# Last stage of an audio tower: column groups of 144, 512 and 512, first norms made one stage earlier, the last tile's router columns first

## The reference, cut to what matters

```python
h = h + attn(layernorm(h), ...)             # its last product: o @ wo.T
x = layernorm(h)
base_out = x @ base_W.T + base_b            # 1024 -> 1024
logits = x @ router_W.T + router_b          # 15 columns
p = softmax(logits); topk_p, topk_i = top_k(p, 8)
w[e] = sum of topk_p with expert_map[topk_i] == e
lora = ((x @ A.T) * w) @ B * 2              # 8 experts of rank 16
h = h + base_out + lora
```

## Time and profile before

| what | value |
|---|---|
| median of three runs | 2515.33 us |
| profiled execution, its own time | 2515.87 us |
| span of the profile | 2514.2 us |
| mean granted TensorE clock | 0.976 |
| TensorE busy | 2367.1 us, 94% of the span |
| VectorE busy | 1807.6 us, 72% |
| ScalarE busy | 1247.0 us, 50% |
| GpSimd busy | 1234.2 us, 49% |

### The profile page before, as it was taken

How to read it: one execution, slowest core, us unless ns; L and a number is a source line. 1 busy time by engine, 2 the same in 40 slices (tenths; PEclk the granted TensorE clock), 3 DMA queues, 4 the chain that set the end, 5 groups by cost and what they waited for, 6 DMA issues and landing times. The chain is left out here.

```text
span 2514.2 us, 45922 instructions
## 1 busy us (share of the span) xinstructions
PE 2367.1 (94%) x14716; PEld 2056.5 (82%) x14716; DVE 1807.6 (72%) x3550; ACT 1247.0 (50%) x3736; POOL 1234.2 (49%) x1012
## 2 busy tenths in 40 slices
PE   8999999988699996899999999989999997999998
PEld 6888878866466676899999999878888875999998
DVE  8865586795456666888888898755776556777775
ACT  5664354441344555899999999823223222111110
POOL 5764686784022224876676767610676553111110
PEclk9999999999899998999999999989999998999999
DMA  7654587666656552211111111197788996211111
GB/s 249 206 178 124 183 260 239 217 217 211 222 168 212 185 177 80 74 43 49 42 49 45 45 46 41 47 309 229 212 254 244 293 274 223 71 68 68 67 67 50
DMA packets 318257, 379.44 MB, mean 151 GB/s; under 512 B 25472, under 2 KB 260480, under 8 KB 317952
## 3 DMA queue, kind: packets, MB, share of 16 engines
q1 hardware_dynamic: 310176, 348.10, 44.2%
q0 software_dynamic: 7184, 25.69, 2.6%
q10 hardware_dynamic: 720, 3.67, 0.4%
HBM read 295.59 MB, written 81.79 MB: 150 GB/s over the span
## 5 line engine op out<-in xcount | busy, mean ns | idle before, releaser
L1518 ACT ACTIVATE attn_prob<-attn_prob,attn_bias 94x94 f32<-94x94 f32 x1024 | 366.9, 361 | 44.4 <-DVE attn_bias L1597 43.1
L740 PE MATMUL up_ps<-up_t_lo,up_s_hi 128*128 128x502 f32 (+1 forms) x840 | 332.9, 396 | 24.4 <-DVE up_t_lo L655 24.4
L741 PE MATMUL up_ps<-up_t_hi,up_s_lo 128*128 128x502 f32 (+1 forms) x840 | 329.2, 392 | 0.0
L742 PE MATMUL up_ps<-up_t_hi,up_s_hi 128*128 128x502 f32 (+1 forms) x840 | 328.5, 391 | 0.0
L506 POOL TENSOR_TENSOR up_both<-up_raw 128x502 f32<-128x502 f32 (+1 forms) x150 | 240.9, 1610 | 114.0 <-DVE up_t_lo L655 83.3
L1638 POOL TENSOR_TENSOR attn_prob<-attn_prob,attn_share 94x752 f32<-94x752 f32 x128 | 187.1, 1462 | 173.7 <-DVE attn_share L1605 173.7
L1886 DVE TENSOR_TENSOR out_t_lo<-early_raw,out_t_hi 128x512 fp32r<-128x512 f32 x168 | 159.1, 951 | 151.1 <-ACT out_t_hi L1865 150.2
L1851 POOL TENSOR_TENSOR early_raw<-early_raw 128x512 f32<-128x512 f32 x120 | 172.1, 1439 | 194.7 <-DMA early_raw<-o_t 193.7
L1865 ACT ACTIVATE out_t_hi<-early_raw 128x512 fp32r<-128x512 f32 x168 | 105.0, 631 | 305.2 <-POOL early_raw L1851 148.8
L655 DVE TENSOR_TENSOR up_t_lo<-up_both,up_t_hi 128x502 fp32r<-128x502 f32 (+1 forms) x150 | 164.3, 1097 | 83.8 <-ACT up_t_hi L564 82.3
L2026 POOL TENSOR_TENSOR ffn_res<-shared_k_t,ffn_bias 128x1024 f32<-128x1024 f32 x24 | 58.7, 2448 | 316.1 <-DVE ffn_o L2148 295.8
(11 more groups left out here) (238 smaller groups left out, 6368.8 us busy)
## 6 DMA issues: line engine op xcount, KB each, us to landing
early_raw<-o_t SPq DMA_DIRECT2D x288, 256.0 KB, 5.0
up_raw<-x_f SPq DMA_DIRECT2D x240, 251.0 KB, 3.3
up_w_raw<-w SPq DMA_DIRECT2D x120, 256.0 KB, 4.0
up_raw<-x_f SPq DMA_DIRECT2D x120, 250.0 KB, 3.6
shared_ring<-wvo SPq DMA_DIRECT2D x96, 256.0 KB, 5.1
o_t<-attn_o_t SPq DMA_DIRECT2D x128, 188.0 KB, 1.9
shared_ring<-wo SPq DMA_DIRECT2D x32, 512.0 KB, 6.6
y<-early_raw POOLq DMA_DIRECT2D x24, 512.0 KB, 3.5
```

What stands on the lines that cost most here:

```text
L740: nc.tensor.matmul(o, sh, tl, start=(kk == 0), stop=False)
L741: nc.tensor.matmul(o, sl, th, start=False, stop=False)
L742: last = nc.tensor.matmul(o, sh, th, start=False, stop=(kk == KH - 1))
L1518: last = nc.scalar.activation(prob[u % NPR][0:SEQ, h, part], prob[u % NPR][0:SEQ, h, part], ACT.Exp, bias=bias[u % 2][0:SEQ, n:n + 1], sca ...
```

## The change

1. **Column groups.** `CUT` goes from [0, 390, 780, 1168] to [0, 512, 1024, 1168], and `base` takes the groups in the order 2, 0, 1: 144 columns (A, router, padding), then 512, then 512. The LoRA product and `ffn_o` now have two groups of 512 in place of 390, 390 and 244.
2. **First norms.** `attn_out` makes the norm's moments of tile 1 ahead of its step 148 and of tile 0 ahead of its step 152, and `xn` of tile 0 as well, into a buffer that outlives the stage and that `c_t` of tile 3 uses before. In `ffn` the first step makes no norm, and the second makes only `xn` of tile 1.
3. **Order of the splits in `ffn`.** ScalarE splits block 0 of `wf` after the first four transposes, and blocks 1 to 8 after both `xt_hi`; VectorE splits blocks 0 and 1 after its first `xt_lo` and 2 and 3 after its second. Before, both engines split blocks 0 to 3 ahead of any of this (VectorE after tile 0's norm).
4. **Residual sums.** GpSimd's first three `res` wait for tile 0's base product.
5. **Last tile.** Its group of 144 columns is done first for all eight blocks (so `base_made` comes then), and the two groups of 512 follow; the LoRA product of the tile before stands after block 4 and not after block 6.

```diff
-def attn_out(nc, d, ow, ox, wf, tiles, h_in):
+def attn_out(nc, d, ow, ox, wf, tiles, h_in, begun):
...
-        c_t = tiles + [mem.sb(f"c_t{i}", [P, DM])[:] for i in range(len(tiles), TILES)]
+        c_t = tiles + [begun.xn] + [mem.sb(f"c_t{i}", [P, DM])[:] for i in range(len(tiles) + 1, TILES)]
...
+            def norm(t):
+
+                dve.wait_ge(taken, PAIR * FINAL_HIGH + t + 1)
+                link.step(1 - t)
+                moments(nc, link, c_t[t], bn, begun.vec[t])
+                link.fill()
+                if t == 0:
+                    dve.wait_ge(lent_stored, 16)
+                    nc.vector.tensor_scalar(begun.xn, c_t[0], begun.vec[0][:, 8:9], begun.vec[0][:, 11:12],
+                                            ALU.subtract, ALU.mult)
+
             for s in range(STEPS):
+                if s in (24 * FINAL_LOW + 4, 24 * FINAL_LOW + 8):
+                    norm(1 - (s - 24 * FINAL_LOW - 4) // 4)
                 dve.wait_ge(hi_done, s + 1)
...
-CUT = [0, 390, 780, FW]
+CUT = [0, DM // 2, DM, FW]
...
                     if not first(t, 3):
                         pool.wait_ge(o_done, t - 2)
+                    else:
+                        pool.wait_ge(base_made, 1)
...
-            for n in range(EARLY):
-                wf.split_hi(act, n)
...
                         act.wait_ge(x_turned, 2 * t + c + 1)
+                        if first(t, 1) and c == 0:
+                            wf.split_hi(act, 0)
...
                     if first(t, 1):
-                        for n in range(EARLY, KM + 1):
+                        for n in range(1, KM + 1):
                             wf.split_hi(act, n)
...
+                        if first(t, 1):
+                            for n in range(2 * c, 2 * c + 2):
+                                wf.split_lo(dve, n)
...
                     if first(t, 1):
-                        for n in range(EARLY):
-                            wf.split_lo(dve, n)
+                        dve.sem_inc(xn_done, 1)
+                    else:
+                        if first(t, 2):
+                            v = begun.vec[1]
+                        else:
+                            v = vec
+                            moments(nc, link, hh, bn, v)
...
-                    for c in range(3):
-                        a, e = CUT[c], min(CUT[c + 1], DM)
+                    for c in range(2):
+                        a, e = CUT[c], CUT[c + 1]
...
-            def base(s, blocks):
+            def base(s, blocks, groups=(2, 0, 1)):
...
-                if n == KM - 1:
+                if n == KM - 1 and 2 in groups:
                     last.then_inc(base_made, 1)
...
-                    base(s, range(0, 4))
+                    ending = isinstance(s[0], int) and s[0] == TILES - 1
+                    groups = (0, 1) if ending else (2, 0, 1)
+                    before = 5 if ending else 7
+                    if ending:
+                        base(s, range(KM), (2,))
+                    base(s, range(0, 4), groups)
...
-                    base(s, range(4, 7))
+                    base(s, range(4, before), groups)
...
-                    base(s, range(7, KM))
+                    base(s, range(before, KM), groups)
```

More of the change, by code:

```diff
@@ L1775, with __init__, moments @@
 ]
-def attn_out(nc, d, ow, ox, wf, tiles, h_in):
+class Begun:
+    def __init__(self, nc, mem):
+        self.xn = mem.sb("xn0", [P, DM])[:]
+        self.vec = [mem.sb(f"vec{i}", [P, 16])[:] for i in range(2)]
+def moments(nc, link, h, bn, v):
+    nc.vector.bn_stats(bn[:, 0:6], h[:, 0:512])
+    link(nc.vector.bn_stats(bn[:, 6:12], h[:, 512:1024]))
+    link.settle()
+    link(nc.vector.bn_aggr(v[:, 8:10], bn[:]))
+    link(nc.vector.tensor_scalar(v[:, 10:11], v[:, 9:10], LN_EPS, None, ALU.add))
+    inv_sqrt(nc, link, v[:, 10:11], v[:, 13:14], v[:, 11:12], v[:, 12:13])
+def attn_out(nc, d, ow, ox, wf, tiles, h_in, begun):
     NT, NB = 5, 8
@@ L1783, in attn_out @@
         ow.more(mem)
-        c_t = tiles + [mem.sb(f"c_t{i}", [P, DM])[:] for i in range(len(tiles), TILES)]
+        c_t = tiles + [begun.xn] + [mem.sb(f"c_t{i}", [P, DM])[:] for i in range(len(tiles) + 1, TILES)]
+        bn = mem.sb("bn", [P, 12])
+        link_sem = mem.sem("link")
+        lent_stored = mem.sem("lent_stored")
         t_hi = [mem.sb(f"t_hi{i}", [P, 4, P], F32R) for i in range(NT)]
@@ L1843, in _ @@
                 sp.sem_inc(h_in[t], 16)
-            sp.wait_ge(h_stored, 16 * TILES)
+            sp.wait_ge(h_stored, 16 * (TILES - 1))
+            sp.wait_ge(lent_stored, 16)
         @block.gpsimd
@@ L1940, in ffn @@
         o = [mem.sb(f"o{i}", [P, DM]) for i in range(2)]
-        xn = [mem.sb(f"xn{i}", [P, DM]) for i in range(2)]
+        xn = [begun.xn, mem.sb("xn1", [P, DM])]
         xt_hi = [mem.sb(f"xt_hi{i}", [P, KM, P], F32R) for i in range(2)]
@@ L2120, in body @@
                     dve.wait_ge(h_in[u % 3], 16 * nth(kb, u, 3))
-                    nc.vector.bn_stats(bn[:, 0:6], hh[:, 0:512])
-                    link(nc.vector.bn_stats(bn[:, 6:12], hh[:, 512:1024]))
-                    link.settle()
-                    link(nc.vector.bn_aggr(vec[:, 8:10], bn[:]))
-                    link(nc.vector.tensor_scalar(vec[:, 10:11], vec[:, 9:10], LN_EPS, None, ALU.add))
-                    inv_sqrt(nc, link, vec[:, 10:11], vec[:, 13:14], vec[:, 11:12], vec[:, 12:13])
-                    if not first(t, 2):
-                        dve.wait_ge(x_turned, 2 * t - 2)
-                    nc.vector.tensor_scalar(xn[u % 2][:], hh[:], vec[:, 8:9], vec[:, 11:12], ALU.subtract,
-                                            ALU.mult).then_inc(xn_done, 1)
-                    if first(t, 1):
-                        for n in range(EARLY):
-                            wf.split_lo(dve, n)
+                    if first(t, 1):
+                        dve.sem_inc(xn_done, 1)
[5 more added lines that the diff above has]
+                            moments(nc, link, hh, bn, v)
+                        if not first(t, 2):
+                            dve.wait_ge(x_turned, 2 * t - 2)
+                        nc.vector.tensor_scalar(xn[u % 2][:], hh[:], v[:, 8:9], v[:, 11:12], ALU.subtract,
+                                                ALU.mult).then_inc(xn_done, 1)
                     if isinstance(t, int) and t == 1:
@@ L2168, in base @@
                         wf.wait(pe, n)
-                    last = three_pass(nc, [ps_o[u % 2][c][:, 0:CUT[c + 1] - CUT[c]] for c in range(3)],
+                    last = three_pass(nc, [ps_o[u % 2][c][:, 0:CUT[c + 1] - CUT[c]] for c in groups],
                                       xt_hi[u % 2][:, n, :], xt_lo[u % 2][:, n, :],
-                                      [w_hi[:, n, CUT[c]:CUT[c + 1]] for c in range(3)],
-                                      [w_lo[:, n, CUT[c]:CUT[c + 1]] for c in range(3)], n == 0, n == KM - 1)
-                if n == KM - 1:
+                                      [w_hi[:, n, CUT[c]:CUT[c + 1]] for c in groups],
+                                      [w_lo[:, n, CUT[c]:CUT[c + 1]] for c in groups], n == 0, n == KM - 1)
+                if n == KM - 1 and 2 in groups:
                     last.then_inc(base_made, 1)
@@ L2215, in body @@
                         wf.wait(pe, KM)
-                    ends = [(CUT[c], min(CUT[c + 1], DM)) for c in range(3)]
+                    ends = [(CUT[c], CUT[c + 1]) for c in range(2)]
                     last = three_pass(nc, [ps_o[u % 2][c][:, 0:e - a] for c, (a, e) in enumerate(ends)], ht_hi[:],
```

10 lines of the change are left out of this document (6 added, 4 removed).

## The result

The changed kernel takes 2541.61 us (median of four runs, 2541.36 to 2542.19) against 2516.32 us for the kernel before on the same chip (2512.67 to 2517.78): a ratio of 1.0105, 95% interval 1.0093 to 1.0117. It is slower, by more than was predicted: 2525 us with a range up to 2533.

What follows compares the result with a forecast made beforehand. TensorE's stream was taken to bound the last stage's steady part, VectorE its start. The terms +20.0 + 3.0 - 10.0 - 3.6 = +9.4 us gave 2525 us from the median, range 2513 to 2533 us.

Steps and rivals of the forecast that it cites:

- Part 2: Stage ahead: the early norms on VectorE delay TensorE near steps 148 and 155; +3.0 us, from 0 to +6.
- The wait at step 155: Stage ahead: TensorE's wait for late operands was to grow from 1.9 to about 4 us.
- Part 3: Start of the last stage: earlier transposes, splits and loads bring tile 1's base product forward; -10.0 us, from -12 to -6.
- I take 1.5: Start of the last stage: tile 2's xn takes 1.5 us beside GpSimd's delayed sums, against 0.82 us alone.
- the start isn't shortened: Rival, start of the last stage: loads come no earlier, only GpSimd's absence gains; -4 for -10, 2531 us; chance 0.10.
- the predicted distance: From the stage ahead's last matmul to tile 1's base product: falls from 39.6 to about 29.5 us.
- the 10 us: Start of the last stage: tile 1's base product starts at 2140.5 us and not 2150.55; -10.0 in the sum.
- the pass of 0.572 us: Last stage: a base pass of the new groups takes 0.037 us more; 552 passes, +20.4 us.
- the term of 0.110 us for 144 columns: Last stage: the short group's share of a pass, added to 2 x 0.231 us for the 512s.
- One sign: Last stage, in the trace after: the 512 behind a 144 starts 0.11 us after it.
- -3.6 predicted: Last tile: hw's transpose waits 1.9 us, not 4.73, and the clock may stay up; between -2.8 and -4.4 us.
- The rival with starved matmuls: Stage ahead: both norms land in full and the low clock comes twice; +9 for +3, 2531 us; chance 0.12.

Runs made afterwards that it cites:

- e5: Kernel after with the statistics buffer bn allocated behind t_lo and not ahead of t_hi; 2527.86 us, ratio 1.0065.
- e6: Kernel before with 512 unused bytes a partition ahead of t_hi; 2514.43 us, ratio 1.0004.
- e13: Kernel before with 256 unused bytes a partition ahead of t_hi; 2515.55 us, ratio 1.0001.
- e11: e10 with the column groups of the change, 144, 512 and 512; 2526.52 us, ratio 1.0043.
- e10: e9 with weight rows 5,120 bytes apart, transposed halves right behind the weights, cuts at 384 and 768; 2501.93 us, ratio 0.9946.
- e2: Kernel before with 64 unused bytes a partition ahead of t_hi; 2525.74 us, ratio 1.0045.
- e4: Kernel after with GpSimd's first three sums waiting for tile 2's norm, not tile 0's base product; 2536.08 us, ratio 1.0092.
- e9: Kernel after with bn behind t_lo, old cuts, first sum waiting for tile 2's norm, next two for the preceding tile's hw transpose; 2507.92 us, ratio 0.9968.
- e3: Kernel after with the old column groups (390, 390, 388) put back; 2521.45 us, ratio 1.0027.
- e8: Kernel after with bn behind t_lo, cuts 456 and 912, first three sums each waiting for their own tile's hw transpose; 2532.22 us, ratio 1.0081.
- e1: Kernel after with the statistics buffer bn allocated 128 bytes a partition and not 64; 2538.34 us, ratio 1.0101.
- e12: e9 with only its cuts moved to 384 and 768; 2504.20 us, ratio 0.9956.

## Why the prediction was wrong

The sign was right and the size wasn't: 16.9 us are missing between +9.4 and +26.3. They are 6.2 in the stage ahead, 6.5 in the start of the last stage, 2.3 in tiles 1 to 23 and 2.0 in where the stage ahead happened to begin, less 0.1 at the end.

**The stage ahead: the step that failed outright.** Part 2 priced what the change puts on VectorE and took TensorE's own matmuls as given ("20 steps of 12 x 0.2266 us"). Its +3.0 is about 0 in most runs with aligned operands (e5 beside e6 and e13) and came in one (e11, +4 beside e10), at step 148, where Part 2 had seen the cover run out. The wait at step 155, which was to grow to 4 us, went away. Slower matmuls give the halves more time: e2, the kernel before with them, doesn't wait there either. But that wait moves by itself too: of the 10 us from 2070 us TensorE is idle for 1.9 before, for 0.6 in e6, for 0.2 in e13 and for none in e10, all four at 0.2267 us. What was there in place of it is a term that the sum didn't have: every allocation of the change ahead of `t_hi` moves it, and with the 64 bytes of this layout 2,016 matmuls come 0.2333 us apart and not 0.2266, as in e2. A sign that 512 columns don't always take the same time stood in the earlier trace rows: 0.234 and 0.2266 us. I put that difference down to the banks, and no run separates it. In the down stage's layout the stationary operand starts 32 bytes off a multiple of 128 from the moving one, so it could be the distance, but that stage wasn't tried in another place; e11's 0.232 us with aligned operands and two banks speaks for the banks.

**The start of the last stage.** Part 3 had the early half right: the transposes, the early splits, the loads right behind the first split, tile 0's base at once. The step that failed is the last, "I take 1.5" for `xn` beside a sum. Only the one large instruction was priced for the collision, and not the small ones of the norm ahead of it. Each of those with two tensor inputs is held until the running sum ends: three times 2.0 to 2.3 us. e4 moves the sums away and gets the predicted distance, 29.61 for about 29.5 us. The rival "the start isn't shortened" had the size (-4 us, measured -3.5) and not the mechanism, since the loads did come earlier (their issue starts 9.1 us after the stage ahead's last matmul, before it was 14.4). That its size fits is luck. And even the 10 us would not have been 10 in the sum: e4 gives 2.9 of its gain back and e9 more, at VectorE's next deadline.

The rows after have 0.15 us for an instruction with one tensor input and 2.02 for one with two, beside the same sum. In the earlier trace rows one `xn` took 2.73 us beside a sum and 0.82 alone, and I took from it a price for `xn` and nothing for the rest. `xn` there and the first row of e4 (2.29 us, 0.22 elsewhere) have one input and were held, so counting inputs isn't enough to call an instruction safe.

**The columns.** The size was nearly right: the pass of 0.572 us was 0.575. No run shows the term of 0.110 us for 144 columns; what the runs showed in its place is 0.112, in the last tile, where they stand alone. 0.003 us by 552 passes is 1.7 of the 2.3 us. One sign was read wrongly: the 512 behind a 144 starts 0.07 us after it and not 0.11, and the missing 0.04 stands behind the first 512, so the sum holds and the place doesn't. e3 shows 21 us between the old groups and the new. e8 shows that a short group costs nothing as such: with 256 columns a pass is 0.535 us, as with 390s, and with 144 it is 0.575.

**The end.** -3.6 predicted, -3.7 measured; the transpose waited 1.74 us for 1.9, and the clock fell only after the first LoRA pass.

**Range and rivals.** The range ended at 2533. It was put together from the gains and losses of the edits that the diff names. The rival with starved matmuls had +9 for the stage ahead, the right total, by a mechanism that didn't occur; its own total of 2531 us lay inside the range.

## What to carry to other kernels

A diff that allocates a buffer moves all that is allocated behind it. If a stage is bound by TensorE, compare the spacing of its untouched matmuls before anything else, and try stationary and moving operands a whole multiple of 256 bytes apart; here 64 bytes more (0.2333 us a matmul for 0.2267) cost 10 us of 2515. When work of GpSimd is put later, list both what runs beside it on VectorE (here small two-input instructions of 0.16 us took 2.0 to 2.3, until the running one ended, and some with one input were held too) and what waits for its result; either list alone gave a wrong answer here. Before you cut a product into uneven groups, measure a pass with the short one (a 256 ahead of two 456s left it at 0.535 us, a 144 ahead of two 512s made it 0.575, and loads came 0.11 us apart at the closest), and give every gap that you close in a start a second look some tiles later.

## What the runs showed of the hardware

In the stage ahead the time between two starts of 512 columns depended on where the stationary operand lay in SBUF, relative to the moving one (and, not separated from it, to the other buffers of the stage). It was 0.2267 us at a multiple of 256 bytes (before, e5, e6, e13), 0.2324 at 128 off (e1) and 0.2333 at 64 off (after, e2), with TensorE never idle and at the full clock for the 200 us. In the last stage, with 384 and 400 columns, a pass of three was 0.535 us in e12 and 0.526 in e10. With two groups of 512 in two banks, aligned, it was 0.232 us a matmul (e11). No run shows the mechanism.

Matmuls with a load each came about 0.11 us apart with 1 and 64 columns (before) and 0.112 with 144 (after, last tile), where the loads came 0.112 apart too. In a pass, 144, 512 and 512 columns took 0.575 us (after), 256, 456 and 456 took 0.535 (e8), and so did 390, 390 and 388 (before).

Beside one addition of 1024 columns on GpSimd (2.3 to 2.4 us) a VectorE instruction with two tensor inputs on one element a partition took 2.0 to 2.3 us and ended with the addition; behind the last one it took 0.16 (after, 2148 to 2155 us). A chain of three moved at the pace of one for each addition. Of instructions with one input, one of 0.15 us was not held (after, 2148.29 us), and two were: `xn`, 2.73 us for 0.82 (before), and `place`, 2.29 for 0.22 (e4).
